# A graph network layer pair: one product of a zero block with 512 constant columns ahead of each tile's own products

## The reference

```python
def spmm(h):
    msg = h[src] * edge_w[:, None]
    agg = jax.ops.segment_sum(msg, dst, num_segments=N)
    return agg + self_w[:, None] * h
h = spmm(x @ W1 + b1); h = relu(batch_norm(h)); h = spmm(h @ W2 + b2)
x = layernorm(x + h)
# then attention over the edges, 8 heads of 16, row = src, col = dst:
scores = einsum('ehd,ehd->eh', q[row], k[col]) / 4 + edge_emb @ eb_w.T + eb_b
attn   = segment softmax of scores over row
out    = segment_sum(attn * v[col], row) @ out_w.T + out_b
x = layernorm(x + out)
```

## Time and profile before

| | us |
|---|---|
| runs of the kernel before | 11748.66, 11755.06, 11759.41 |
| median | 11755.06 |
| the profiled execution, first to last instruction (span) | 11509.7 |
| `spmm1`, first to last L1569 | 426 to 3014 |
| `spmm2`, first to last L1569 | 3133 to 6720 |
| the expansion, first to last L1866 | 6913 to 9508 |

### The profile page before, as it was taken

How to read it: one execution, slowest core, us unless ns; L and a number is a source line. 1 busy time by engine, 2 the same in 40 slices (tenths; PEclk the granted TensorE clock), 3 DMA queues, 4 the chain that set the end, 5 groups by cost and what they waited for, 6 DMA issues and landing times. The chain is left out here.

```text
span 11509.7 us, 203325 instructions
## 1 busy us (share of the span) xinstructions
PE 7087.3 (62%) x39548; PEld 6173.5 (54%) x39549; DVE 5806.8 (50%) x16002; ACT 2519.6 (22%) x8525; POOL 6063.8 (53%) x6650
## 2 busy tenths in 40 slices
PE   6687878777566566666666644444444446773774
PEld 5576777777455555555555523333333335662664
DVE  7433333333355455555555554444444445668777
ACT  8100000000122222222222210000000003442885
POOL 6465655555544444444443465555555555553665
PEclk8655555565656666666666667777777778996997
DMA  1233333333311111111111132222222225552553
GB/s 37 76 87 81 85 85 82 85 84 83 103 35 32 32 33 32 31 32 32 32 31 31 32 83 84 88 87 85 86 88 85 84 85 146 137 138 58 154 154 103
DMA packets 1057786, 868.49 MB, mean 75 GB/s; under 512 B 214824, under 2 KB 950424, under 8 KB 1057736
## 3 DMA queue, kind: packets, MB, share of 16 engines
q0 software_dynamic: 179664, 437.87, 12.6%
q1 hardware_dynamic: 643032, 319.49, 10.5%
q10 hardware_dynamic: 235040, 110.58, 3.4%
HBM read 578.04 MB, written 287.84 MB: 75 GB/s over the span
## 5 line engine op out<-in xcount | busy, mean ns | idle before, releaser
L1492 POOL DMA_INDIRECT spmm_rows<-h_table,spmm_index_ring x3136 | 3082.1, 983 | 3130.5 <-PE bank L1569 2099.5
L1569 PE MATMUL bank<-spmm_rows,spmm_hot 128*128 x6660 | 2067.8, 412 | 550.2 <-DVE region_ab L1542 440.3
L1845 POOL DMA_INDIRECT kv_sorted<-expand_payload,expand_where_ring x1568 | 1508.9, 962 | 1114.3 <-issue 1066.1
L1569 PEld LDWEIGHTS bank<-spmm_rows,spmm_hot 128*128 128x128 f32 x6660 | 1620.1, 296 | 641.8 <-issue 623.5
L1866 PE MATMUL bank<-region_ab,expand_hot_t 128*128 x3336 | 1097.8, 486 | 1392.6 <-DVE expand_hot_t L1884 1121.2
L1542 DVE TENSOR_TENSOR region_ab<-region_ab,bank 128x128 f32 x3330 | 957.7, 288 | 1873.3 <-remote 902.8
L1866 PEld LDWEIGHTS bank<-region_ab,expand_hot_t 128*128 128x128 f32 x3336 | 775.4, 245 | 1577.1 <-issue 1451.3
L1901 DVE SCALAR_TENSOR_TENSOR expand_payload<-expand_payload,region_c,bank 128x256 f32 x1668 | 801.6, 481 | 1236.3 <-issue 397.3
L745 PE MATMUL bank<-spmm_beside_hot_hi,spmm_beside_hot_lo 128*128 128x98 bf16 x1568 | 563.1, 359 | 1044.5 <-ACT spmm_beside_next_slot L782 818.8
L782 ACT COPY spmm_beside_next_slot<-bank 128x98 f32<-128x98 f32 x1568 | 379.0, 242 | 2690.6 <-PE bank L745 1296.6
L704 DVE CUSTOM_DVE_ANT_0 spmm_beside_junk<-bank,spmm_beside_hot_hi 128x98 f32<-128x98 f32 x1568 | 448.1, 323 | 959.4 <-DMA bn_cols<-in_L_gnn_bn_var_dram 690.4
(11 more groups left out here) (353 smaller groups left out, 12601.3 us busy)
## 6 DMA issues: line engine op xcount, KB each, us to landing
score_k_rows<-kv_sorted SPq DMA_DIRECT2D x420, 288.0 KB
mix_mixed<-kv_sorted SPq DMA_DIRECT2D x420, 256.0 KB
spmm_beside_attr_sb<-in_edge_attr_dram ACTq DMA_DIRECT2D x390, 256.0 KB
spmm_rows<-h_table,spmm_index_ring POOLq DMA_INDIRECT x3136
kv_sorted<-expand_payload,expand_where_ring POOLq DMA_INDIRECT x1568
kv_sorted<-spmm_beside_blank SPq DMA_DIRECT2D x1, 15232.0 KB
kv_sorted<-spmm_beside_blank SPq DMA_DIRECT2D x98, 136.0 KB
h_table<-region_ab SPq DMA_DIRECT2D x28, 448.0 KB
```

The costliest lines, as they stand in the source:

```text
L1492: nc.gpsimd.indirect_dma_start(rows[:, h * HALF + k, :], None, table, bass.IndirectOffsetOnAxis(ap=index_ring[:, h, k:k + 1], axis=0)).the ...
L1569: last = nc.tensor.matmul(sums_of(k), hot[:, k // HOTS % HOT_GROUPS, k % HOTS, :], tile_of(rows, place[k % HALF]), start=True, stop=True)
L1845: nc.gpsimd.indirect_dma_start(kv_sorted, bass.IndirectOffsetOnAxis(ap=where_ring[:, h, k:k + 1], axis=0), payload[:, h * HALF + k, 0:ROW] ...
```

## The change

A helper is added that multiplies a block of zeros (128x128, bf16) with the first 512 columns of a table of small constants (bf16) and writes the result to a bank of PSUM that nobody reads at that time. In the sparse products it is called once per tile, after the waits for the one-hots and the adds and ahead of the wait for `arrived`. In the expansion it is called four times per group, after the next group's `spread_keys` and ahead of the wait for the group's one-hots. Beside it, `until_window` and `pairs_done` become unsigned 16-bit numbers instead of 32-bit ones.

```diff
-        until_window, window_place = node_rows[UNTIL_ROW:UNTIL_ROW + 1, :], node_rows[PLACE_ROW:PLACE_ROW + 1, :]
-        pairs_done = sb("pairs_done", [1, E_HALVES], I32)
+        until_wide, window_place = node_rows[UNTIL_ROW:UNTIL_ROW + 1, :], node_rows[PLACE_ROW:PLACE_ROW + 1, :]
+        until_window = until_wide.bitcast(U16)[:, 0:S_TILES]
+        pairs_done = sb("pairs_done", [1, E_HALVES], U16)
...
-        node_at, steps_row = until_window, node_d.bitcast(BF16)[:, 0:S_TILES]
+        node_at, steps_row = until_wide, node_d.bitcast(BF16)[:, 0:S_TILES]
...
+        def keep_busy(into):
+
+            nc.tensor.matmul(into[:, 0:512], zeros_bf[:, 0:P], iota_rows[:, :, :].rearrange("p a b -> p (a b)")[:, 0:512], start=True, stop=True)
...
+                SPARE_BANK = 3 if name == "spmm1" else 5
...
                             if k % 2 == 0:
                                 need(pe, added, t - 2)
+                            keep_busy(bank[SPARE_BANK])
                             pe.wait_ge(arrived, until[k % HALF])
...
                         node = loaded(mybir.EngineType.PE, node_d[0:1, bass.ds(i * TURN + j * GROUP, GROUP)], GROUP, NT - 1, CLAMPED)
+                        for m in range(GROUP):
+                            keep_busy(bank[6])
                         pe.wait_ge(hot_ready, g + 1)
```

More of the change, by code:

```diff
@@ L4 @@
 from concourse import mybir
-F32, I32, BF16 = mybir.dt.float32, mybir.dt.int32, mybir.dt.bfloat16
+F32, I32, BF16, U16 = mybir.dt.float32, mybir.dt.int32, mybir.dt.bfloat16, mybir.dt.uint16
 ALU, ACT, AX = mybir.AluOpType, mybir.ActivationFunctionType, mybir.AxisListType
```

## The result

| | kernel before | changed kernel |
|---|---|---|
| time, median of 4 runs each, us | 11757.2 (11748.7 to 11759.5) | 12176.8 (12138.0 to 12198.6) |
| profiled execution: span, us | 11509.7 | 12136.3 |
| mean granted clock | 0.694 | 0.770 |

The ratio is 1.0356 (95% interval 1.0336 to 1.0375), 419 us more. The two traces differ by 627 us, more than the runs do: the traced execution of before was 245 us shorter than its runs, that of the change wasn't (12138.0 against a span of 12136.3). Comparisons of stretches with the old trace are thus too large by about a third. The experiments supply pairs from one chip.

The account below looks back on a forecast made before the run. TensorE's clock and GpSimd gathers waiting on TensorE were taken to bound the sparse products, VectorE's one-hots to delay the expansion. Terms: -102 (spmm2) - 80 (spmm1) = -182 us, giving 11573 us; range 11350 to 12040, own range 11450 to 11720.

Parts of the forecast that it names:

- The price of a product: One 512-column bf16 product on TensorE: 0.42 us at 1.2 GHz, 0.22 us at 2.4 GHz, weight load taken as free.
- That the constant columns raise the clock: In spmm1 and spmm2, what the array streams sets the granted clock, not the busy share; the added product supplies it.
- the rival that doubted it: A product with a zero block leaves the granted clock unchanged, W near 0.3 in spmm2: 12313 us, chance 0.05.
- the 0.75 named as the sign in spmm2: If the forecast holds, the spmm1 and spmm2 stretches have a granted clock of 0.75 or more.
- The share at the upper level in spmm2: Share W of spmm2 tiles at the upper clock level: 0.73, so 1.335 us a tile against 1.40, 102 us less.
- one stall of about 6 us per half: In spmm2, TensorE's idle time is one stall per half, 5028.6 to 5034.8 in the trace, while the clock falls back.
- The first rival: The stall decides: W 0.5 costs 172 us more in spmm2, some 50 more in spmm1; 11977 us, chance 0.33.
- the rule of the Trainium skill: Loops with a wait each round start cold again; the product leaves each half's low part in place and makes it dearer.
- Nothing hidden in spmm2: In spmm2 the 0.67 us idle per tile is mostly the long stall, where no product stands; none counted as hidden.
- spmm1: Clock mostly up, TensorE's 7.9 us well below GpSimd's 12.5 us floor per eight windows; 80 us less, half the possible gain.
- The expansion: Four products per group stand between `spread_keys` and a wait for VectorE, 0.88 us at the upper level; taken as 0.
- The 16-bit rows: As many register loads as before, 1673 on TensorE's queue; taken as 0, at most 100 us either way.

## Why the prediction was wrong, step by step

**The price of a product** was right: 0.42 and 0.22 us forecast, 0.40 and 0.23 in the rows above; a tile of spmm2 takes 1.81 and 1.09 us (median between sum products at either level; 1.89 and 1.13 forecast).

**That the constant columns raise the clock** was right, and the rival that doubted it wrong: 0.63 to 0.71 in spmm2, 0.57 to 0.74 in spmm1 on one chip. It rose less than the 0.75 named as the sign in spmm2.

**The share at the upper level in spmm2** is the term that was mis-sized. I took W = 0.73, from 4.3 us of work at the lower level behind one stall in 8.5 tiles. Measured was 0.51: in the trace of the change beside the 16-bit rows, TensorE works at the lower level for 1522 us of spmm2, 7.8 us in each of the 196 halves. My own formula gives 172 us more for W = 0.5, and 148 were measured between two traces of one chip. The step that failed before it is the reading of one round as all of them. In the trace of before the same count gives 1759 us, 9.0 a half, where the round of the earlier trace rows had 5.4; and "one stall of about 6 us per half" is not the rule there. Of the 209 stretches of eight tiles in that spmm2, 39 have a pause of 5.5 us or more, and 101 have two or more pauses above 1.5 us. The round shown above has such a second pause (2.48 us ahead of 5037.59). The first rival was built on this, and the rule of the Trainium skill that the prediction named beside it (TensorE: Matmul & The Clock Gate, section "HAM oscillation — how this bites in real kernels") held in spmm2: the waits stayed and with them the low part of each half. On a chip without stalls W is 0.79 with the same products and they cost 42 us; hidden under the loads 0.92, and they gain 201.

**Nothing hidden in spmm2** was right for the place that the change chose, and the place was the fault: the sequencer's loads leave 2.5 us a half in which eight products fit, and moving them there took 141 us back with stalls.

**spmm1** failed in sign: 80 us less forecast, 127 more measured. I took the clock as mostly up and so TensorE as far below GpSimd's floor. W was 0.53, and TensorE's work grew by as much as the stage did (131 us), which speaks for TensorE, and not GpSimd's floor, still setting the pace. Without stalls, the step is right in kind: 32 us less.

**The expansion** was forecast at nothing, with the four products in VectorE's wait. The wait covers them, even at the lower level over two groups. I had looked for a cost on TensorE's queue alone and none in the stall, behind which TensorE comes back 1 us later. The stage takes 123 us more, and the cause stays open.

**The 16-bit rows** were forecast at 0 within 100 us, because their number stays. They cost 33 us with stalls and 104 without. The count of loads in the earlier trace rows was the wrong thing to look at: one load of eight 16-bit values takes 1.92 us instead of 0.59. That most of it is hidden where TensorE waits out a stall anyway is a guess: no trace of the kernel before stands beside one of the 16-bit rows on one chip.

**The base.** The trace lay 245 us below the runs. Kept as an offset it did no harm to the sum, but it was a sign: the kernel before took 11534 us on one chip with stalls and 11770 on others. Had I known of 9260 us without them, the stalls would have been the first thing to price.

The forecast of 11573 us was 604 below the result, the range (to 12040) 137. By terms the miss is 250 us in spmm2 (102 less forecast, 148 more measured), 207 in spmm1, 123 in the expansion and 33 for the 16-bit rows, 613 in all, with the stages measured on another chip than the result. Rival 1 at 11977 had the right side, spmm2 and 50 us of spmm1; the rest of spmm1 and the expansion neither case had.

## What to carry to other kernels

Filler work for the clock belongs where the engine's sequencer is busy or its queue is held up anyway (here under the register loads), not ahead of a product that is due; price it at the level that holds behind each stall. Don't count on a second helping to pay as the first may: here the first cost nothing without stalls, the next 0.12 us each. Read how often a round repeats before one round is priced for all of them. Before a change is sized against waits of unknown cause, find out whether they are there on another chip.

## What the runs showed of the hardware

- The same kernel takes 9.26 ms on some chips and 11.5 to 11.8 on others. Nearly all of it lies in the three stages with GpSimd's indirect DMAs (with the 16-bit rows alone 2064, 2626 and 1983 us against 2631, 3746 and 2710); the part behind them takes 1989 and 1994.
- A busy TensorE can stand at the lower level for 3 ms: with products of 8 columns spmm2 had a busy share of 0.9 and a clock of 0.50; with 512 columns, also without stalls, the clock was 0.88. In spmm1 the products of 8 columns didn't lower it (0.58 to 0.64).
- A zero block as weights is no obstacle to the upper level: with two such products in each place the clock was 0.99 in spmm1.
- Register loads from a 16-bit row are dearer than from a 32-bit row: 1922 ns against 589 for eight values on TensorE.
